# First feed-forward layer: the clamp of each gate tile's code moves from VectorE to GpSimd

## The reference, cut to what matters

```python
def act_qdq(x):                       # 16-bit codes, one scale for the whole tensor
    scale = max(max(abs(x)) / 32767, 1e-12)
    return clip(round(x / scale), -32768, 32767) * scale
def fixed_qdq_u16(x):
    return clip(round(x * 65536), 0, 65535) / 65536
x    = act_qdq(x)
up   = act_qdq(x @ dequant(w_up).T)       # 2048 tokens x 384
gate = act_qdq(x @ dequant(w_gate).T)
sig  = fixed_qdq_u16(sigmoid(gate))       # the clamp in question
gate = act_qdq(gate * sig)
o    = act_qdq(gate * up)
return o @ dequant(w_down).T
```

## Time and profile before

| | us |
|---|---|
| median of 3 runs | 1343.97 (1343.85 to 1346.62) |
| profiled execution | 1353.68 |
| its span, first to last instruction | 1351.9 |
| TensorE, VectorE, ScalarE, GpSimd busy | 1222.1, 830.8, 653.7, 285.1 |

### The profile page before, as it was taken

How to read it: one execution, slowest core, us unless ns; L and a number is a source line. 1 busy time by engine, 2 the same in 40 slices (tenths; PEclk the granted TensorE clock), 3 DMA queues, 4 the chain that set the end, 5 groups by cost and what they waited for, 6 DMA issues and landing times.

```text
span 1351.9 us, 27707 instructions
## 1 busy us (share of the span) xinstructions
PE 1222.1 (90%) x10063; PEld 960.2 (71%) x10063; DVE 830.8 (61%) x1781; ACT 653.7 (48%) x1338; POOL 285.1 (21%) x381
## 2 busy tenths in 40 slices
PE   5999971889999899999999999889999999989999
PEld 2555620458788889887887888478889866657777
DVE  4888678564555566657777565456564477764242
ACT  2666686445434334444454444233434457755553
POOL 4877300120003142330000014043340021200000
PEclk9999995999999999999999999999999999999999
DMA  9000010501142113103106101032102000000000
GB/s 326 2 1 2 11 69 0 210 1 63 35 177 84 56 53 102 49 27 147 67 1 249 68 7 48 24 101 67 47 18 87 1 2 2 3 2 1 1 16 16
DMA packets 42898, 75.86 MB, mean 56 GB/s; under 512 B 3848, under 2 KB 33680, under 8 KB 41872
## 3 DMA queue, kind: packets, MB, share of 16 engines
q1 hardware_dynamic: 38672, 65.69, 13.4%
q0 software_dynamic: 4096, 8.40, 2.1%
HBM read 59.78 MB, written 14.29 MB: 55 GB/s over the span
## 4 chain that ended last, share of the span: by engine, by line
PE 76%; DVE 13%; ACT 5%; issue 3%; DVEq 1%; DMA 1%; POOL 0%; ACTq 0%; SPq 0%; POOLq 0%
PE bank L1869 7%; PE bank L1880 7%; PE bank L1865 7%; PE bank L1924 5%; PE bank L1611 4%; PE bank L1856 4%; PE bank L1934 3%; PE bank L1616 3%; PE bank L1618 3%; PE bank L1617 3%; PE bank L1681 2%; PE bank L1849 2%; PE bank L1851 2%; PE bank L1850 2%; PE bank L1697 2%
## 5 line engine op out<-in xcount | busy, mean ns | idle before, releaser
L2127 ACT ACTIVATE SC<-bank 128x512 f32<-128x512 f32 x192 | 114.3, 595 | 223.1 <-PE bank L1865 124.0
L2214 DVE SCALAR_TENSOR_TENSOR SC<-bank,SM,SC 128x512 f32<-128x512 f32 x128 | 95.8, 748 | 123.2 <-PE bank L1869 102.5
L1880 PE MATMUL bank<-A,SC 128*128 x1024 | 137.0, 277 | 7.9 <-DVE SC L2214 7.1
L1869 PE MATMUL bank<-X,SC 128*128 128x128 f32 x1024 | 136.8, 277 | 4.4 <-DVE SC L2489 3.9
L1865 PEld LDWEIGHTS bank<-X,SC 128*128 128x128 f32 x1024 | 126.1, 192 | 20.0 <-issue 13.0
L1865 PE MATMUL bank<-X,SC 128*128 128x128 f32 x1024 | 136.1, 276 | 3.7 <-ACT SC L2111 2.5
L1880 PEld LDWEIGHTS bank<-A,SC 128*128 128x128 f32 x1024 | 125.4, 192 | 17.4 <-issue 16.5
L1869 PEld LDWEIGHTS bank<-X,SC 128*128 128x128 f32 x1024 | 124.5, 192 | 6.9 <-DVE SC L2489 6.7
L1924 PE MATMUL bank<-A 128*128 128x128 f32 x736 | 100.4, 280 | 16.0 <-DVE A L2639 10.5
L1924 PEld LDWEIGHTS bank<-A 128*128 128x128 f32 x736 | 90.1, 193 | 21.1 <-ACT A L2152 13.0
L2790 POOL TENSOR_SCALAR A<-A,CC 128x256 f32<-128x256 f32 (+1 forms) x128 | 55.4, 451 | 189.7 <-DVE A L2306 102.2
(11 more groups left out here) (340 smaller groups left out, 2530.7 us busy)
## 6 DMA issues: line engine op xcount, KB each, us to landing
A<-in_moe SPq DMA_DIRECT2D x36, 768.0 KB, 10.5
A<-xs SPq DMA_DIRECT2D x20, 256.0 KB, 3.7
ys<-A SPq DMA_DIRECT2D x20, 256.0 KB, 2.3
BW<-in_l1f SPq DMA_DIRECT2D x2, 2048.0 KB, 7.3
BW<-in_l2f SPq DMA_DIRECT2D x1, 3456.0 KB, 10.7
BW<-in_l1c SPq DMA_DIRECT2D x1, 3072.0 KB, 16.7
BW<-in_l3f SPq DMA_DIRECT2D x1, 2816.0 KB, 9.8
A<-in_l1c SPq DMA_DIRECT2D x1, 2560.0 KB, 8.7
```

The costliest lines, as they stand in the source:

```text
L1869: m = e.matmul(at["pu"].ap[:, cut(q)], wx[:, cut(4 + q)], x, start=True, stop=True)
L1880: m = e.matmul(o, at["h"].ap[:, cut(q)], W[:, bass.ds(r + (1024 + 128 * q), 128)], start=k == 0 and q == 0, stop=k == 1 and q == 3)
L2127: e.activation(at["h"].ap, at["pg"].ap, ACT.Gelu_apprx_tanh).then_inc(at["gelu"][0], 1)
L2214: return e.scalar_tensor_tensor(out=o, in0=a, scalar=s, in1=b, op0=o1, op1=o2)
```

## The change

Stage g3 of each of the twelve gate tiles is issued by GpSimd in place of VectorE, with the same operation, operands and constants. Its semaphore is one of its own, `f0_pool`. Its place on the list is the same, and g4 waits for it as before. VectorE keeps g4 (the product) and g5 (the maximum).

```diff
             def f3():
                 at = step("g3", s=u["s"], prev=u["t"])
-                at["t"] = u["t"] = tick("f0_vec")
+                at["t"] = u["t"] = tick("f0_pool")
...
@@ VectorE
-                elif kind == "g3":
-                    w.wait_ge(*at["prev"])
-                    ts(at["s"].ap, at["s"].ap, 192.0, 192.0 + 65535.0 / 65536, ALU.add, ALU.min).then_inc(at["t"][0], 1)
...
@@ GpSimd
+                elif kind == "g3":
+                    w.wait_ge(*at["prev"])
+                    e.tensor_scalar(at["s"].ap, at["s"].ap, 192.0, 192.0 + 65535.0 / 65536, ALU.add, ALU.min).then_inc(at["t"][0], 1)
```

## The result

The change makes the kernel slower: 1362.46 us (median of 5 runs, 1359.74 to 1363.04) against 1345.06 (5 runs, 1343.85 to 1346.62). The ratio is 1.0125, interval 1.0113 to 1.0136, which is +15 to +18 us. I had forecast 1354.1, which is +10.1, and a range of 1349 to 1364. The sign and the new configuration pairs were right. One of the 12 runs of a later kernel (clamps 0 to 2 on GpSimd) took 1818.6 us at a granted clock of 0.64, where the others had 0.98, and is left out of that kernel's figures.

What follows compares the result with a forecast made beforehand. VectorE's chain to the fourth all-reduce was taken as the bound. Clamps leaving it, but three exposed configuration pairs of 6.6 us and alternating clamps and products, moved that all-reduce from 216.76 to 226.9: 1343.97 + 10.1 = 1354.1 us, range 1349 to 1364.

Steps and rivals of the forecast that it cites:

- new configuration pairs: In GpSimd's queue, four added pairs of configuration instructions where clamps and all-reduces alternate, three of them exposed.
- this phase: Gate-tile stretch, measured from ScalarE's first g0 to its first product tile; forecast +10.1 us, with nothing behind it changing.
- 2.6 us at best: At the fourth all-reduce, the gain of a perfect change: it would end at 214.2 instead of 216.8.
- A pair lasts 6.6 us: On GpSimd, each configuration change taken as a 6.6 us code load, from a 128 KB load row; limits 0.1 and 15.6.
- B: Rival at GpSimd's configuration changes: each pair takes 8 us or more, time 1358 to 1387 us; chance 0.14.
- C: Rival at GpSimd's configuration changes: each pair takes at most 3.3 us, time 1341.4 to 1344 us; chance 0.08.
- One clamp costs 0.68 us: On GpSimd, a 512-column clamp, extrapolated from tensor_scalars of 256 and 128 columns; ends 0.47 and 1.27 us.
- the lock: GpSimd's clamp and VectorE's product exclude each other, 1.28 us a tile; loss +10.1 us with it, +8.6 without.
- The walk: Step-by-step timing of the gate tiles by effective durations, putting the fourth all-reduce's end at 226.9 against 216.76, +10.1 us.
- the third pair: On GpSimd between the up scale's all-reduce and clamp 5: forecast to end at 212.2 us, only then can clamp 5 run.
- Rival D: GpSimd bound by its own speed: short pairs of 2.8 us, clamps of 1.27 us, +4.0, time 1348.0; chance 0.06.
- A: The forecast itself: pairs of 5 to 8 us, loss +5.4 to +14.4 us, most likely 1354.1; chance 0.72.

Runs made afterwards that it cites:

- the fast form: The changed kernel with its GpSimd clamps altered from add-min to multiply by 1, add 192, upper bound left out: 1354.21 us against 1344.60 before, ratio 1.0061.
- Without pairs: All-reduces replaced by elementwise GpSimd instructions; ratios against the kernel before: 0.9996 with VectorE clamps, 1.0006 with GpSimd add-min, 0.9979 with GpSimd multiply-add.
- the kernel with the trial instructions: The kernel before plus nine extra, unread GpSimd tensor_scalars near the start; 512-column ones with a minimum took 1.93 to 1.97 us, no kernel time given.

## Why the prediction was right in sign and short in size

1. *What this phase loses, the kernel loses in full.* Right: +16.86 us of phase, +16.8 of time.
2. *Taking 12 clamps from VectorE is worth 2.6 us at best.* Right: 2.71, once nothing else is in the way.
3. *Four new pairs, at 184, 198.6, 205.6 and 220, the first hidden.* Right in number and in place on the list; by the clock they start at 183.6, 200.4, 206.9 and 227.1, later because the clamps ahead of them are slower. *A pair lasts 6.6 us.* Right as a mean: 6.95 to 7.14 us ahead of elementwise instructions, 5.77 to 6.14 ahead of the all-reduce. That the row chosen for it, a load of 128 KB in 6.6 us, is the reason, no run shows; I call the agreement luck. The 5.95 us of the Trainium skill (GPSIMD Engine Reference, section 2.1, Instruction dispatch) agrees with the second kind. Rivals B (8 us and more) and C (under 3.3) fall.
4. *One clamp costs 0.68 us, between 0.47 and 1.27.* This is the term that failed. It measures 1.91, outside both ends. I bounded it with instructions of another pair of operations and treated the size as the only difference. With clamps of 0.61 us the same kernel loses 8.81 us (forecast 10.1, 8.6 without the lock), with 1.91 it loses 16.86. The 8.05 between them are that term. The walk itself shows it too. With 1.91 for each clamp, seven in a row behind the third pair and everything else as predicted, its fourth all-reduce ends at 197.9 + 1.91 + 6.6 + 0.35 + 6.6 + 13.37 + 6.6 + 0.35 = 233.7, which is +16.9 (an estimate from the walk's terms). Rival D, too slow by its own speed, had the right suspicion at too small a price, and it was not a rival of the pairs, it came on top.
5. *Clamp and product alternate.* Wrong in form. Behind the third pair, seven clamps of 1.907 us ran in 13.28 us, 1.897 each, so products did not hold them up; the products took 1.09 us in place of 0.68, and the 0.4 us more are hidden behind the clamps. A short clamp is held up, 1.11 to 1.21 us for 0.62, but with the fast form five of them behind the third pair ran in 3.81 us, 0.76 each, where I had 1.28.
6. *The profiled execution would be 1363.8, and the difference between it and the runs carries over.* It came to 1362.68 with a loss of 7 us more than assumed, because before's profiled execution was slow elsewhere. The phase, not the spans, is what should be compared.
7. *Range 1349 to 1364.* The time, 1362.46, lies in it by luck. What I called most likely (A, chance 0.72) ended at 1358.4. The range went beyond that only for pairs of more than 8 us (B, 0.14), and no pair took more than 7.14. A clamp price outside both of my ends brought the time to where B would have put it.

The two causes make each other worse. Without pairs, slow clamps cost 33.58 - 29.42 = 4.16 us, since most of GpSimd's 12 x 1.9 lies under ScalarE's work. With pairs the clamps start late, 7 of them stand in one chain, and the same slowness costs 8.05.

## What to carry to other kernels

Before work goes to GpSimd, list what stands on its queue around it: an elementwise instruction between two all-reduces cost two changes of configuration of 6 to 7 us each, though the profile of before showed them only as records of nanoseconds under long idle times. Price the instruction by its own pair of operations, not by another of the same name: here 0.61 or 1.91 us for the same 128x512. And a queue that sat idle for 12 us between instructions is not free capacity if its idle time can't be split.

## What the runs showed of the hardware that I had not expected

- GpSimd's tensor_scalar at 128x512 float32: 0.61 to 0.62 us for multiply-add, add-multiply and multiply-multiply, 1.49 for an addition alone, 1.93 to 1.97 with a minimum. A second operation can make it faster: add and multiply by 1 is 0.62, add alone 1.49.
- What a product of VectorE loses beside a clamp of GpSimd depends on when it starts, not on how long the clamp lasts. In the kernel after, the product at 215.81 starts right behind a clamp of 1.91 us (215.77) and takes 1.10 us for 0.68, and with the fast form one takes the same 1.10 beside a clamp of 0.62 (213.16). With every second clamp on GpSimd, the products at 209.38 and 212.10 start 1.17 and 0.55 us behind one and take 0.68. So a clamp of 1.91 us holds a product up for some 0.5 us of its length at most (an estimate from these starts). The Trainium skill, SBUF — State Buffer, "Who interferes with whom", says that the second one waits until the first has finished. The product at 215.81 does not agree with that: it was done at 216.91, while its clamp ran to 217.68. For GpSimd behind VectorE the rule nearly holds: 0.5 to 0.6 us more beside a product of 0.60.
- The first pair of the program, at 5.9 us in the kernel with the trial instructions, was over by 8.76, when a load released the clamp: 2.9 us at most, where all later ones took 5.8 to 7.1. Why it is shorter was not tried.
